# A decoder layer in one kernel: a third of each large product moved ahead in the units of its cross attention, and other orders at its head and tail

## The reference

```
x = x + attention(norm(x))                 # 128 heads of 4 features, latent down and up projections, a rope-like part of 64
x = x + cross_attention(norm(x), context)  # 32 query heads, 8 key/value heads of 16, rotary positions, softmax
x = x + ffn(norm(x))                       # base product + bias + a mixture of 8 low-rank experts, top 2 by a gate
```

## Time and profile before

| | us |
|---|---|
| runs: 828.11, 828.34, 830.26; median | 828.34 |
| profiled execution, its own time | 826.78 |
| its span | 824.5 |
| TensorE busy | 793.0 |
| VectorE busy | 628.6 |
| ScalarE busy | 582.7 |
| GpSimd busy | 590.9 |

### The profile page before, as it was taken

One profiled execution on the slowest core, in us unless ns is written; L12 is line 12 of the kernel. 1 busy time (PEld: TensorE's weight loads), 2 busy tenths in 40 slices (PEclk: granted clock), 3 DMA queues, 4 the chain that ended last, 5 costly groups with the idle time before them and its releaser, 6 DMA issues.

```text
span 824.5 us, 17894 instructions
## 1 busy us (share of the span) xinstructions
PE 793.0 (96%) x5641; PEld 391.9 (48%) x5641; DVE 628.6 (76%) x1190; ACT 582.7 (71%) x1072; POOL 590.9 (72%) x535
## 2 busy tenths in 40 slices
PE   5999999999999999999999999999999899999987
PEld 3464444444444444444444444444444444555444
DVE  6766676676677788776788876778878888888766
ACT  8757777777777777777777777778765655666551
POOL 7967999999988888887888887878655634222111
PEclk9999999999999999999999999999999999999999
DMA  9344355533434333343333344352321000000001
GB/s 344 124 172 142 93 142 161 162 98 89 104 107 120 90 79 93 89 128 100 100 81 97 83 119 107 92 158 63 88 61 48 27 2 2 14 14 13 18 15 39
DMA packets 52176, 75.80 MB, mean 92 GB/s; under 512 B 10256, under 2 KB 34096, under 8 KB 51616
## 3 DMA queue, kind: packets, MB, share of 16 engines
q1 hardware_dynamic: 52128, 75.23, 32.8%
HBM read 38.69 MB, written 19.40 MB: 70 GB/s over the span
## 4 chain that ended last, share of the span: by engine, by line
PE 87%; DVE 4%; ACT 3%; issue 2%; SPq 2%; DMA 1%; POOL 0%; DVEq 0%; ACTq 0%
PE PS L1567 40%; PE PS L1639 7%; PE PS L1606 7%; PE PS L1640 7%; PE PS L1501 6%; PE PS L1654 5%; PE PS L1740 2%; PE PS L1832 2%; PE PS L1679 1%; PE PS L1798 1%; PE PS L1616 1%; PE PS L1688 1%; PE PS L1839 1%; PE PS L1817 1%; PE PS L1849 1%
## 5 line engine op out<-in xcount | busy, mean ns | idle before, releaser
L1567 PE MATMUL PS<-XTh,W 128*128 128x512 f16 x1024 | 346.0, 379 | 0.0
L656 POOL TENSOR_TENSOR Pl<-PR,Ph 128x512 f16<-128x512 f32 x254 | 285.8, 1156 | 28.4 <-ACT Ph L938 28.4
L931 ACT ACTIVATE PR<-PS 128x512 f32<-128x512 f32 x256 | 152.8, 597 | 131.7 <-PE PS L1640 124.9
L1125 DVE TENSOR_REDUCE mneg<-PS 128x4 f16<-128x512 f32 x256 | 171.6, 685 | 35.3 <-PE PS L1606 33.4
L1567 PE MATMUL PS<-XTl,W 128*128 128x512 f16 x512 | 193.6, 378 | 0.0
L1113 DVE SCALAR_TENSOR_TENSOR QS<-PS,QC 64x512 f16<-64x512 f32 x256 | 175.5, 685 | 20.8 <-ACT QC L848 16.7
L848 ACT ACTIVATE QC<-PS 64x512 f16<-64x512 f32 x256 | 150.7, 589 | 9.2 <-PE PS L1567 4.3
L1567 PEld LDWEIGHTS PS<-XTh,W 128*128 128x128 f16 x1024 | 96.6, 97 | 118.8 <-issue 25.9
L938 ACT ACTIVATE Ph<-PR 128x512 f16<-128x512 f32 x256 | 139.3, 617 | 0.0
L1606 PEld LDWEIGHTS PS<-KC,QC 112*128 112x128 f16 x1024 | 78.4, 97 | 63.5 <-issue 2.7
L1606 PE MATMUL PS<-KC,QC 112*128 112x128 f16 x1024 | 99.4, 219 | 0.9 <-ACT QC L848 0.8
(11 more groups left out here) (236 smaller groups left out, 1034.1 us busy)
## 6 DMA issues: line engine op xcount, KB each, us to landing
Wraw<-in_wqr SPq DMA_DIRECT2D x32, 512.0 KB, 4.8
QS<-QC SPq DMA_DIRECT2D x64, 256.0 KB, 3.2
head_outputs<-OS SPq DMA_DIRECT2D x256, 40.0 KB
q_content_parts<-stg SPq DMA_DIRECT2D x12, 256.0 KB, 2.9
k_content_parts<-stg SPq DMA_DIRECT2D x12, 256.0 KB, 3.1
QC<-q_content_parts SPq DMA_DIRECT2D x116, 24.0 KB
KC<-k_content_parts SPq DMA_DIRECT2D x29, 96.0 KB
xs<-in_x SPq DMA_DIRECT2D x8, 256.0 KB, 4.8
```

The source lines that it names most:

```text
L656: nc.gpsimd.tensor_tensor(Pl[:, 4 * j.s + b], PR[:, b], Ph[:, 4 * j.s + b], ALU.subtract).then_inc(s_pl, 1)
L931: nc.scalar.activation(PR[:, b, :], PS[:, bB[b % 2], :], ACT.Exp, scale=ATT_SCALE).then_inc(s_e, 1)
L1125: nc.vector.tensor_reduce(mneg[:, j.p, j.s, :, b], PS[:, bA[b % 2], :].rearrange("p (j k) -> p j k", j=GH), AX.X, ALU.max, negate=True).th ...
L1567: last = mm(PS[:, bQ[c], :], wt[:, j.w, k, c * P:(c + 1) * P], xt[:, k, sl], start=(i == 0), stop=(i == 3 * KT - 1))
```

## The change

- Head: GpSimd normalises tiles 1, 3, 5, 7 and ScalarE 0, 2, 4, 6, in another order with its copies. The key rope's latents come ahead of the four expansions, in bank 1, and their copies ahead of three context copies; the second half of the first query product waits for them.
- Cross attention: the first pass of a unit's large product goes between `turn` and `x_back`. `outputs_turn` goes ahead of `x_rough` where r = 2 (in unit 5 it stays). In unit 8 the late output goes ahead of `x_back`, the turn of normalised tile 0 behind `x_scores`, and its high and low copies later too. In unit 7 `x_outputs` goes behind the query rope. The second key rope goes from unit 1 to unit 5.
- Tail: base of tile 5 in bank 2, of 6 in bank 3, of 7 in bank 7; the first pass of `base(5)` in unit 31, and the last `low_turn` ahead of the last pass of `base(7)`.

```diff
         def base_bank(v):
-
-            return bF[1] if v < B - 2 else 2 + v % 2
+            return {B - 3: 2, B - 2: 3}.get(v, bF[1])
...
             return [(CS[:, w], 2 + t, RD * w, t) for t in range(2) for w in range(2)] + \
-                [(KS, 2 + t, RD * t, t) for t in range(2)]
+                [(KS, bQ[1], RD * t, t) for t in range(2)]
...
-                if i >= 2:
-                    b = 2 * i + 1
-                    pool.wait_ge(n_sd[0], i + 1)
-                    nc.gpsimd.tensor_scalar(xn[:, b, :], xs[:, b, :], rstd[:, 0, b:b + 1], mv[:, 0, b, 0:1],
-                                            ALU.mult, ALU.add).then_inc(s_pp, 1)
+                b = 2 * i + 1
+                pool.wait_ge(n_sd[0], i + 1)
+                nc.gpsimd.tensor_scalar(xn[:, b, :], xs[:, b, :], rstd[:, 0, b:b + 1], mv[:, 0, b, 0:1],
+                                        ALU.mult, ALU.add).then_inc(s_pp, 1)
...
-            for b in range(4):
-                normed(b)
+            normed(0)
+            normed(2)
             x_high(0)
+            normed(4)
             x_high(1)
             act.wait_ge(s_wd, 16)
             nc.scalar.activation(wd_h[:], wd_raw[:], ACT.Copy, scale=WS).then_inc(s_wdh, 1)
-            normed(4)
             x_high(2)
+            normed(6)
             x_high(3)
-            normed(6)
...
             for i in range(4):
                 up_high(i)
+            latent_high(4)
+            latent_high(5)
             for k in range(1, KT):
                 ctx_high(k)
-            latent_high(4)
-            latent_high(5)
...
-                if r == 1:
+                if r == 1 and u != 8:
                     norm_high(2, b - 2, bF[0], s_f)
...
                 x_exps(u, 1)
+                if u == 8:
+                    norm_high(2, 0, bF[0], s_f)
...
                 if half:
                     dve.wait_ge(s_kvr, 1)
-                    dve.wait_ge(s_xqa, 2)
+                    dve.wait_ge(s_xqa, 3)
...
                 if r == 1:
-                    norm_low(2, b - 2, bF[0])
+                    if u != 8:
+                        norm_low(2, b - 2, bF[0])
...
                     x2(b - 1, bF[1])
-                if 0 <= u - 1 < NU:
+                if u == 8:
+                    norm_low(2, 0, bF[0])
+                if 0 <= u - 1 < NU and u != 7:
                     x_outputs(u - 1)
...
                         nc.vector.tensor_tensor(qr[:], rt[:, 0], rt[:, 1], ALU.add).then_inc(s_xqa, 1)
+                if u == 7:
+                    x_outputs(u - 1)
...
                     x1(3)
-                if u == 1:
+                if u == 5:
                     k_rope(1)
...
             pe.wait_ge(s_id, 1)
             for b in range(B):
-                if b in (5, 7):
-                    pe.wait_ge(s_pp, b // 2 - 1)
-                else:
-                    pe.wait_ge(n_xn[0], b + 1 if b < 5 else 6)
+                pe.wait_ge(s_pp if b % 2 else n_xn[0], b // 2 + 1)
...
 
-            pe.wait_ge(s_pp, 3)
-            for i in range(4):
-                up_content(i)
-
             for k in range(KT):
                 for n, (wt, xt) in enumerate(down):
                     for t in range(2):
-                        last = mm(PS[RD * t:RD * (t + 1), 2 + t, :], wt[:, k, 2 * LAT:], xt[:, k, t * HALF:(t + 1) * HALF],
+                        last = mm(PS[RD * t:RD * (t + 1), bQ[1], :], wt[:, k, 2 * LAT:], xt[:, k, t * HALF:(t + 1) * HALF],
                                   start=(k == 0 and n == 0), stop=(k == KT - 1 and n == 2))
                         if k == KT - 1 and n == 2:
                             last.then_inc(s_c, 1)
 
+            pe.wait_ge(s_pp, B // 2 + 1)
+            for i in range(4):
+                up_content(i)
+
             for c in range(4):
+                if c == 1:
+                    pe.wait_ge(s_cl, 6)
                 for k in range(KT):
                     project(job(c // 2), c % 2, k)
...
+                    pe.wait_ge(s_oT, v + 1)
+                    pe.wait_ge(s_xl, 4)
+                last = parts(bank, O2h[:, v % 2], O2l[:, v % 2], woh, wol, 0, DM, (s_oTl, v + 1), turns)
+                if turns[-1] == 2:
+                    last.then_inc(s_o2, 1)
 
             last_read = {}
 
@@ -1864,12 +1875,15 @@
                         last = nc.tensor.transpose(PS[:, bank, k * S:(k + 1) * S], O2[:, v % 2, k * P:(k + 1) * P], ident[:])
                     last.then_inc(s_ot, 1)
...
+                        pe.wait_ge(n_tl[1], v + 1)
+                        take(bF[0], s_xqp, v + 1)
+                        pe.wait_ge(s_wxl, 1)
+                    last = parts(bF[0], Ah1[:, v % 2], Al1[:, v % 2], Wxh, Wxl, 0, DM, None, turns)
+                    if turns[-1] == 2:
+                        last.then_inc(s_xq, 1)
 
             def late_output(v):
                 if v == B // 2:
@@ -1888,30 +1902,41 @@
                     low_turn(b - 3)
                 if 0 <= u + 2 < NU:
                     turn(u + 2)
+                if r == 0:
...
+                    elif u != -1:
+                        query(b + 1, (0,))
+                if r == 1 and 0 <= b - 3 < B:
+                    take(bF[1], s_x3, b - 2)
+                    base(b - 3, 0)
+                if r == 2 and 0 <= b - 2 < B:
+                    take(bF[1], s_ge, b - 1)
+                    gate(b - 2, bF[1], (0,))
+                if r == 3 and 0 <= b - 1 < B:
+                    take(bF[1], s_x2, b)
+                    project_outputs(b - 1, bF[1], (0,))
+                if u == 8:
+                    late_output(LATER[u])
                 if 0 <= u - 2 < NU:
                     x_back(u - 2)
-                if u in LATER and u <= 8:
+                if u in LATER and u < 8:
                     late_output(LATER[u])
                 if r == 0 and u != -1:
-                    query(b + 1)
+                    query(b + 1, (1, 2))
                 if r == 1:
                     if 0 <= b - 3 < B:
-                        v = b - 3
-                        take(bF[1], s_x3, v + 1)
-                        for n in range(3):
-                            base(v, n)
-                        lora(v)
-                    norm_turn(2, b - 2, bF[0])
-                if r == 2:
-                    if 0 <= b - 2 < B:
-                        v = b - 2
-                        take(bF[1], s_ge, v + 1)
-                        gate(v, bF[1])
+                        base(b - 3, 1)
+                        base(b - 3, 2)
+                        lora(b - 3)
+                    if u != 8:
+                        norm_turn(2, b - 2, bF[0])
+                if r == 2 and 0 <= b - 2 < B:
+                    gate(b - 2, bF[1], (1, 2))
+                    outputs_turn(b - 1, bF[0])
                 if r == 3:
                     if 0 <= b - 1 < B:
-                        v = b - 1
-                        take(bF[1], s_x2, v + 1)
-                        project_outputs(v, bF[1])
+                        project_outputs(b - 1, bF[1], (1, 2))
                     if u == -2:
                         pe.wait_ge(s_oe, NH)
                         keep_clock(2)
@@ -1943,6 +1968,8 @@
                     query(1)
                 if 0 <= u < NU:
                     x_scores(u)
+                if u == 8:
+                    norm_turn(2, 0, bF[0])
                 if 0 <= u - 1 < NU:
                     x_weigh(u - 1)
 
@@ -1951,14 +1978,12 @@
             low_turn(B - 3)
             x_back(NU - 2)
             x_weigh(NU - 1)
...
-            take(bF[1], s_x3, B - 2)
-            base(B - 3, 0)
+            base(B - 3, 1)
             x_back(NU - 1)
             norm_turn(2, B - 2, bF[0])
             outputs_turn(B - 1, bT7)
             gate(B - 2, bG)
             project_outputs(B - 1, bP7)
-            base(B - 3, 1)
             base(B - 3, 2)
             lora(B - 3)
             base(B - 2, 0)
@@ -1969,10 +1994,11 @@
             gate(B - 1, bG)
             base(B - 2, 2)
             lora(B - 2)
-            for n in range(3):
-                last = base(B - 1, n)
-            last.then_inc(s_o2, 1)
+            take(bF[1], s_x3, B)
+            base(B - 1, 0)
+            base(B - 1, 1)
             low_turn(B - 1)
+            base(B - 1, 2).then_inc(s_o2, 1)
             lora(B - 1)
...
```

37 lines of the change are left out of this document (19 added, 18 removed).

## The result

The changed kernel takes **822.08 us** (median of 12 executions, 821.79 to 825.54). The kernel before, run beside it, has a median of **827.12** over 12 (825.99 to 830.26), not the 828.34 of the three that the prediction started from. The ratio is 0.9942, 95% interval 0.9933 to 0.9952: faster by 4.8 us (4.0 to 5.5).

The account below looks back on a forecast made before the run. TensorE, busy 793.0 of 824.5 us, was taken as the bound, so only its holes and slow clock pay. Terms: 1.5 + 1.25 - 1.35 + 1.3 + 1.9 - 0.2 - 0.8 - 0.5 + 0.5 = 3.6, giving 824.7; range 822.9 to 826.6.

Parts of the forecast that it names:

- The baseline: Whole kernel: the profiled 826.78 us and the median 828.34 of three runs, to which the profile's differences were carried over.
- Head, 1.5: Start of kernel: tiles shared with GpSimd gain 0.44, key rope latents ahead of the expansions 1.09; 1.5 taken, bounds 0.4 to 1.6.
- Unit 3, 1.25: Cross attention, unit 3: the hole of 1.03 goes and the turn back no longer waits for OW; 1.25 us gained.
- Key rope, -1.35: Second key rope in unit 5: 3.4 us beside GpSimd's splits, so query 3 waits about 1.35 for the low part.
- Units 8 and 9, 1.3: Wait with drain, slow clock and late output give 3.3; new waits of 0.4, 1.2 and 0.4 cost 2.0.
- First thirds, 11 x 0.17 = 1.9 - 0.2: First thirds ahead of the turn back fill 0.17 in 11 units; unit 11's late low part takes 0.2.
- r = 1, -0.8: Units 12, 16, 20, 24: the base third delays the turn back, and the normalised tile's turn waits 0.2 for the rope's bank.
- r = 2, -0.5: Units 13, 17, 21, 25: the outputs' turn ahead of the rough scores waits for VectorE's outputs; -0.13 each.
- Unit 11: Unit 11: the low part of tile 4 comes 0.2 late, since VectorE has units 9 and 10 closer together.
- Tail, 0.5: End of kernel: only the last step counts, the wait of 0.37 and the turn's remaining latency go; 0.5 us.
- the rope never ran alone: Rival, unit 5's key rope: GpSimd's splits slip by a microsecond, 1.25 more is gained, 823.4 us; chance 0.17.
- The clock's fall in unit 7: Rival: a new hole in unit 7 or unit 9 takes TensorE to 1.2 GHz once; price 1.22, 825.9 us; chance 0.18.

Follow-up runs that it names:

- changed_again: The changed kernel run once more without edits, on the same chip as the runs beside it; 822.37 us, ratio 0.9938 to the kernel before.
- head_alone: The kernel before with only the head's edits, nothing of the cross attention changed; 825.77 us, ratio 0.999.
- unit8_alone: The kernel before with only the edits of units 7 to 9, second key rope still in unit 1; 825.46 us, ratio 0.9977.
- thirds_undone: The changed kernel with the large products whole again behind the turn back, in all units but the last; 824.00 us.
- tail_undone: The changed kernel with the tail of the kernel before, the loop's first thirds kept; 822.61 us.
- early_clock_before: The kernel before with 30 unread transposes ahead of the first normalised tile and 4 more ahead of tiles 2, 4 and 6; 825.14 us, ratio 0.9986.
- the first group: The first set of follow-up runs, told beside the kernel before at 827.01 us: head_alone, unit8_alone, unit8_filled and thirds_undone.
- high_early: The changed kernel with unit 8's high copy ahead of ScalarE's copy of weighed values and the low part ahead of VectorE's maxima; 822.17 us.
- unit8_filled: The kernel before with eight products nobody reads in unit 8, ahead of the late output, filling TensorE's wait; 827.26 us, ratio 1.000.

## Why the prediction came out as it did

**The baseline: the step that failed, with the largest share.** "I take differences from the profile over to the median", and the median was that of three executions, 828.34. 64 later executions of the same kernel have medians of 826.7 to 827.4. 827.1 - 3.6 would have been 823.5, inside the range. So 1.2 of the 2.6 by which I was wrong is the sample, and I had its warning in hand: the profiled execution was 1.6 lower. By itself that would still have been inside the range; the 0.8 of the span and the 0.7 around it, told next, bring 823.5 to 822.0.

**Around the span.** 2.3 us lay around it before (median 2.4 in those executions), 1.7 in all 12 of the changed kernel, but 2.75 in one of the five of changed_again: 0.7 that no sum over instructions can have. It isn't tied to an edit that I can name: head_alone and unit8_alone have 2.5, thirds_undone and tail_undone 1.7, early_clock_before 1.7 though its code is that of before but for the transposes. Open.

**The span: 3.6 predicted, 4.4 in the profiles.** Term by term:

- *Head, 1.5.* The key rope's part is right (1.09 said, 1.0 measured). The tiles' part (0.44) is not there: up to the second half of the latents the new order is 0.7 later than the old at the late clock (19.84, 19.18) and 1.5 later at the early one (19.79, 18.31). The prediction read the 16 transposes of the earlier trace rows as held by ScalarE's tiles; they ran one behind the other at the clock's lower level. The trace's 1.58 is 0.88 by 60 us, made up with the clock's early rise, and 0.7 of small waits in the heads loop that differ between executions of unchanged code: from 60 to 594 us it is 533.97 before, and 533.27 to 534.34 in the other profiles of the first group. The size came out right by luck. (The upper level began by 13 us in 10 of the 12 profiles of the new order and in one of three of the old; whether the order brings that isn't shown.)
- *Unit 3, 1.25.* 1.30.
- *Key rope, -1.35.* -1.14 in unit 7 with whole products. "So I take 3.4": 3.8 measured. Row and rule of the Trainium skill ("GPSIMD Engine Reference", the specifications: VectorE and GpSimd share their SBUF interfaces) pointed the right way, and this case's runs agree: 3.81 beside the splits, 2.00 without.
- *Units 8 and 9, 1.3.* 1.63 in sum, with two parts wrong: the slow clock, where it fell, was worth 0.66, not 1.22, and what came in its place cost less (0.17 + 1.09 + 0.21 against 0.4 + 1.2 + 0.4).
- *First thirds, 11 x 0.17 = 1.9 - 0.2.* The most mis-sized term, in both directions. In the eight units where the third is ready it is 0.30, since the steps around the turn back shrink as well as the wait: 2.4. In units 7 and 11 its sign is wrong, -0.5 each: the turn back lost its cover (0.22), and what the unit before had won was waited out. 1.3 in all, plus 0.65 in unit 30, which I had booked in the tail at 0.5.
- *r = 1, -0.8:* -0.4. The wait for the rope's bank is there at its forecast size: in unit 20 the turn of the normalised tile starts 1.06 behind the last product (744.89 to 745.95), before it was 0.86 (748.12 to 748.98). But the turn back behind a third costs 0.1 less here too, which the sum hadn't counted. *r = 2, -0.5:* -0.50, by the mechanism foreseen: 0.59 of waiting for the outputs.
- *Unit 11.* "The low part is 0.2 late" was 0.26 with a whole product; then the third's 0.5 on top.
- *Tail, 0.5:* 0.73, of which 0.28 the last step.

Against their forecasts, the eight ready thirds gave 1.1 more, r = 1 0.4, units 8 and 9 0.3, the tail and unit 28 0.4, head and unit 3 0.1; units 7, 11 and 15 gave 1.4 less. What is left of all these is 0.8. The mechanisms that the sum missed are the lost cover, the waited-out gain, and the clock as a matter of chance. **The rivals:** the rope never ran alone by itself. The clock's fall in unit 7, given 0.18, is real and a matter of chance: it came in one of seven profiles with that hole. Three of the twelve executions of the changed kernel had a mean granted clock of 0.998 or less, with spans of 821.7 to 823.8 where the others have 820.1 to 821.6; in changed_again it was one of five, with 820.7. Of the 64 of the kernel before it was 48. So falls are rarer in the changed kernel, but how much of the gain that is can't be read from them: before, the spans have a median of 824.6 at 1.00 and 824.0 at 0.998. In none of the profiles did a fall begin in an r = 2 unit.

## What to carry to other kernels

Measure the baseline as often as the change, and when the profiled execution and the median of a few runs disagree by nearly half of what you forecast (1.6 and 3.6 here), widen the range by it. Moving part of a product ahead of a small step pays where the part can start (0.30 here). Where it must wait itself, it costs what the small step did under that wait (0.22), and what was won just before is waited out (0.3): look in each unit, not in the steady one, at when its operand is due and when its bank is free. Before moving an instruction of VectorE with inputs in SBUF, look at what GpSimd does in its new seat; one wait of GpSimd's, on a split that nobody needed yet, was worth more (1.8 in its unit) than the move itself.

## What the runs showed of the hardware

- VectorE's instructions beside GpSimd's splits: 1.54 against 0.69 us (128x512, two SBUF inputs), 0.86 against 0.38 (128x256), 1.18 against 0.54 (one SBUF input and per-row scalars), 1.06 against 0.23 (128x64). GpSimd's own split took 1.49 against 1.16.
- Behind the same hole of 1.80 us in the same code, TensorE's clock stayed at its upper level in six profiles and fell to the lower in one; behind the hole of 1.76 in unit 8 of the old order it fell in two of three. A fall cost 1.69, 1.67 and 1.59 where TensorE had little to wait for behind it (unit 7 in high_early, unit 2 in tail_undone, the tail in unit8_filled), and 0.66 in unit 8 of the kernel before, where it had.
- In the head, the same transposes ran with the clock's rise anywhere from 11 to 19 us of the span; in three profiles (thirds_undone, tail_undone, unit8_filled) it fell again at 14.3 to 14.4, until 17.7 to 17.9.
